# A chunked state-space scan: the next chunk's first segment sum and decay rows issued earlier, fp32r products regrouped

## The reference

```python
dAc = jnp.cumsum(dA, axis=-1)
seg = dAc[..., :, None] - dAc[..., None, :]
Lm = jnp.where(mask, jnp.exp(seg), 0.0)
Y_diag = jnp.einsum('bcqhn,bcshn,bhcqs,bcshp->bcqhp', Cm, Bm, Lm, xdt)
decay_states = jnp.exp(dAc[..., -1:] - dAc)
states = jnp.einsum('bcqhn,bhcq,bcqhp->bchpn', Bm, decay_states, xdt)
...
new = s + d[:, :, None, None] * carry
...
Y_off = jnp.einsum('bcqhn,cbhpn,bhcq->bcqhp', Cm, prevs, jnp.exp(dAc))
y = rmsnorm(y * jax.nn.silu(z), norm_w)
return y @ out_proj_w
```

## Time and profile before

| | us |
|---|---|
| runs: median of 3 (lowest to highest) | 1455.87 (1454.92 to 1456.91) |
| the profiled execution, its own time | 1456.05 |
| its span in the trace | 1453.9 |
| TensorE busy | 1385.4 (95%) |
| VectorE busy | 960.9 (66%) |
| ScalarE busy | 641.2 (44%) |
| GpSimd busy | 488.0 (34%) |

### The profile page before, as it was taken

The page is one execution under the profiler, slowest core; times in us unless marked ns, Lnnn a source line. Parts: engine busy times, 40 slices in busy tenths (PEclk is TensorE's granted clock), DMA queues, the critical chain, the costliest instruction groups (busy, mean ns, idle before and its releaser), DMA issues.

```text
span 1453.9 us, 20837 instructions
## 1 busy us (share of the span) xinstructions
PE 1385.4 (95%) x7268; PEld 1110.3 (76%) x7268; DVE 960.9 (66%) x1322; ACT 641.2 (44%) x1123; POOL 488.0 (34%) x479
## 2 busy tenths in 40 slices
PE   6899999989999997999999999999998789999997
PEld 4677777756666665888888888888886689999996
DVE  6879697789999996233333333233346879999996
ACT  4444454555555554221111121121212258888885
POOL 2612121247777675111010111010101336556652
PEclk9999999999999999999999999999999879999999
DMA  9133122833222222410000001020037724444433
GB/s 203 60 114 106 70 88 77 245 112 119 102 102 102 103 103 83 156 30 15 30 29 14 29 14 32 26 83 26 0 114 245 271 53 72 76 80 71 74 53 44
DMA packets 84360, 124.47 MB, mean 86 GB/s; under 512 B 27695, under 2 KB 44079, under 8 KB 84272
## 3 DMA queue, kind: packets, MB, share of 16 engines
q1 hardware_dynamic: 71488, 103.62, 21.8%
q0 software_dynamic: 8736, 18.62, 7.7%
q10 hardware_dynamic: 4048, 1.10, 0.3%
HBM read 81.37 MB, written 43.78 MB: 86 GB/s over the span
## 4 chain that ended last, share of the span: by engine, by line
PE 55%; DVE 2%; issue 1%; DMA 1%; ACT 1%; ACTq 0%; POOL 0%; DVEq 0%; POOLq 0%
PE fin_bank L1951 52%; PE fin_bank L2087 1%; DMA out_dram<-result_rows,put_idx 1%; PE fin_bank L2106 1%; PE fin_bank L2019 0%; PE fin_bank L2007 0%; PE fin_bank L2075 0%; DVE ff_w_lo L1736 0%; DVE onehot L1844 0%; ACT gu_hi L1632 0%; DVE fi_bn L1771 0%; DVE gu_lo L1863 0%; ACT ff_w_hi L1610 0%; ACTq L1337 0%; POOL out_dram L1564 0%
## 5 line engine op out<-in xcount | busy, mean ns | idle before, releaser
L1698 DVE TENSOR_TENSOR ff_prod<-ff_prod,fin_bank 128x512 f32<-128x512 f32 x64 | 44.0, 688 | 263.2 <-PE fin_bank L1951 263.2
L1951 PE MATMUL fin_bank<-ff_hT_hi,ff_w_hi 128*128 128x512 f32 x512 | 202.7, 396 | 3.2 <-DVE ff_w_lo L1706 3.2
L1951 PE MATMUL fin_bank<-ff_hT_lo,ff_w_hi 128*128 128x512 f32 x512 | 202.5, 395 | 0.0
L1951 PE MATMUL fin_bank<-ff_hT_hi,ff_w_lo 128*128 128x512 f32 x512 | 202.5, 395 | 0.0
L1450 POOL TENSOR_TENSOR ff_w_lo<-ff_stage,ff_w_hi 128x1024 fp32r<-128x1024 f32 (+1 forms) x24 | 56.5, 2356 | 410.6 <-ACT ff_w_hi L1600 406.2
L544 DVE SCALAR_TENSOR_TENSOR conv_acc<-raw,conv_w,conv_acc 128x512 f32<-128x512 f32 x144 | 115.7, 804 | 41.8 <-ACT raw L350 35.6
L649 PE MATMUL pj_bank<-hT_hi,w_in_hi 128*128 128x512 f32 x336 | 135.8, 404 | 6.9 <-POOL w_in_lo L297 4.2
L1585 ACT ACTIVATE ff_prod<-fin_bank 128x512 f32<-128x512 f32 x64 | 38.3, 598 | 231.2 <-PE fin_bank L1951 231.2
L649 PE MATMUL pj_bank<-hT_lo,w_in_hi 128*128 128x512 f32 x336 | 133.6, 398 | 0.0
L649 PE MATMUL pj_bank<-hT_hi,w_in_lo 128*128 128x512 f32 x336 | 132.7, 395 | 0.0
L1863 DVE TENSOR_TENSOR gu_lo<-wx,gu_hi 128x1408 fp32r<-128x1408 f32 (+1 forms) x79 | 124.9, 1620 | 1.6 <-ACT gu_hi L1632 1.6
(11 more groups left out here) (320 smaller groups left out, 3198.3 us busy)
## 6 DMA issues: line engine op xcount, KB each, us to landing
cv_rows<-cst SPq DMA_DIRECT2D x12, 1024.0 KB, 4.3
cv<-cv_rows SPq DMA_DIRECT2D x16, 768.0 KB, 4.2
zs_rows<-zst SPq DMA_DIRECT2D x8, 1024.0 KB, 6.5
zs<-zs_rows SPq DMA_DIRECT2D x16, 512.0 KB, 5.2
wx<-in_L_ffn_Wg_dram SPq DMA_DIRECT2D x8, 704.0 KB, 8.3
wx<-in_L_ffn_Wu_dram SPq DMA_DIRECT2D x8, 704.0 KB, 8.4
w_raw<-in_L_attn_in_proj_w_dram SPq DMA_DIRECT2D x32, 128.0 KB, 3.5
x<-_attn_hidden_states_dram SPq DMA_DIRECT2D x16, 256.0 KB, 5.4
```

What stands on the lines that cost most here:

```text
L1698: eng.tensor_tensor(prod[c][:, :], prod[c][:, :], up_ps[c][:, :], ALU.mult).then_inc(s["prod"], 1)
L1951: mm = eng.matmul(ps, w[a], x[b], start=first and i == 0, stop=last and i == 2)
```

## The change

In the lists of TensorE and ScalarE the first segment sum `seg(c + 1, 0)` with its exponentials and the first decay rows `cum_rows(c + 1, 0)` with theirs are issued at the end of pass c in place of the start of pass c + 1; on TensorE they stand right behind `out_proj(e, 1)` and ahead of the transposes `rows(c + 1)`. `seg(c, 2)` stands ahead of `diagonal(c, 0)` in place of behind it. On VectorE the two scores 0 and 1 follow each other, and `decayed_c(c, 0)` comes after both. No instruction is added or removed, and nothing changes on GpSimd and SyncE.

```diff
--- before.py
+++ after.py
@@ -938,12 +938,12 @@
                        .then_inc(s["wo_hi"], 1)
 
             rows(0)
+            exps(0, 0)
+            cum_exp(0, 0)
             for c in range(TILES + 2):
                 e, f = c - 1, c - 2
                 now, late, later = c < TILES, 0 <= e < TILES, 0 <= f
                 if now:
-                    exps(c, 0)
-                    cum_exp(c, 0)
                     exps(c, 1)
                 if c == 0:
                     out_high(0, HPG)
@@ -963,8 +963,11 @@
                     high(c, 0)
                     if c + 1 < TILES:
                         rows(c + 1)
+                        exps(c + 1, 0)
                 if late and now:
                     h_squares(e)
+                if c + 1 < TILES:
+                    cum_exp(c + 1, 0)
 
         @block.vector
         def _(eng):
@@ -1071,8 +1074,8 @@
                     gate(e, 1)
                 if now:
                     score(c, 0)
+                    score(c, 1)
                     decayed_c(c, 0)
-                    score(c, 1)
                 if c == 0:
                     out_low(0, HPG)
                 if late:
@@ -1217,19 +1220,19 @@
                 last.then_inc(s["h2T"], 1)
 
             rows(0)
+            seg(0, 0)
+            cum_rows(0, 0)
             for c in range(TILES + 2):
                 e, f = c - 1, c - 2
                 now, late, later = c < TILES, 0 <= e < TILES, 0 <= f
                 if now:
-                    seg(c, 0)
-                    cum_rows(c, 0)
                     b_dot_c(c, 0)
                     seg(c, 1)
                 if late:
                     out_proj(e, 0)
                 if now:
+                    seg(c, 2)
                     diagonal(c, 0)
-                    seg(c, 2)
                     carried(c, 0)
                 if late and now:
                     row_sums(e)
@@ -1241,6 +1244,9 @@
                     cum_rows(c, 1)
                 if late:
                     out_proj(e, 1, None if now else row_sums)
+                if c + 1 < TILES:
+                    seg(c + 1, 0)
+                    cum_rows(c + 1, 0)
                 if c == TILES:
                     turn_h2(f)
                 if now:
```

## The result

| | us |
|---|---|
| kernel before, 5 runs beside it: median (lowest to highest) | 1456.20 (1454.92 to 1457.49) |
| changed kernel, 5 runs: median (lowest to highest) | 1464.39 (1462.77 to 1464.83) |
| ratio, 95% interval | 1.0054, 1.0043 to 1.0065 |
| the profiled execution of the changed kernel, its span | 1464.39, 1462.3 |

A forecast was written before the change was run, and what follows sets the result against it. The prediction took a ring through TensorE, VectorE and GpSimd, ending with VectorE's squares, as the bound; 14 passes x 0.67 = 9.4 us on 1456.05 gave 1465.4, median 1465.2, own range 1462 to 1469, whole range 1454 to 1485.

The forecast's parts named there:

- The ring: One scan pass, from TensorE through VectorE's outcome, GpSimd and VectorE's squares back to TensorE's L1208; claimed to set its 17.32 us.
- The moved products: On TensorE, three fp32r products of 0.23 us ahead of the transposes; xdt starts later but ends as before, costing nothing.
- ScalarE's order: Moved exponentials ahead of h_squares on ScalarE make GpSimd's L861 wait, and the first L818 starts 0.67 us later.
- VectorE's order: Second score waits for its exponentials, decayed_c arrives 0.06 us ahead of the first L818, low is held; pass grows 0.67.
- the signs: Timeline marks of a right forecast, among them the second score waiting some 1.5 us and TensorE idle about 1.2 before L1208.
- The sum: Over the scan, 14 passes x 0.67 = 9.4 us slower, with nothing added for the opening.
- The opening: Chunks 0 and 1 of the scan, with waits of their own; given zero with 1 us to either side.
- The first rival: decayed_c comes after the first L818 starts, so both it and low are held; 1476 or 1485 us, chance 0.33.
- The fourth: Rival: the delays fit into the margins and the first L818 waits less than computed; 1456 us, chance 0.07.
- the second rival: low on VectorE isn't held and ends 0.16 us before its old time; -2.2 us, 1453.9, chance 0.09.
- the third rival: TensorE ends the pass; 0.33 us of wait and 0.22 of stretches go, 7.7 us faster, 1448, chance 0.06.

The follow-up runs named there:

- e5: The kernel before with only seg(c, 2) moved ahead of diagonal(c, 0) on TensorE, one fp32r stretch fewer; 1454.90 us, ratio 0.9987.
- e4: The changed kernel with h_squares back ahead of the exponentials and decayed_c back between the scores, products still moved; 1454.04 us, ratio 0.9982.
- e6: The changed kernel with GpSimd's two L818 products replaced by memsets that read nothing, leaving out the D x x term; 1451.45 us, ratio 0.9963.
- e1: The changed kernel with ScalarE's h_squares back ahead of the next chunk's exponentials; 1467.24 us, ratio 1.0074.
- e3: The changed kernel without VectorE's swap, decayed_c back between the two scores; 1445.99 us, ratio 0.9933.
- e2: The kernel before with VectorE's swap alone, the second score ahead of decayed_c; 1469.53 us, ratio 1.0091.
- e7: e3 with seg(c, 2) behind diagonal(c, 0) again, one fp32r stretch more; 1452.88 us, ratio 0.9969.

## Why the prediction was right, point by point

**The ring through GpSimd and VectorE's squares, not TensorE, ends the pass: right.** e5 and e4 shorten or move TensorE's work and leave the pass at 17.27; e6 touches only GpSimd and takes 0.83 off the changed kernel's.

**The moved products cost nothing: right.** Counted from the outcome, xdt began 0.69 later, as computed, and ended within 0.01 of its old place (3.18 against 3.19), and e4 has the old pass.

**ScalarE's order delays L818 by 0.67: right in size** (7.76 against 7.09 behind the outcome), and low ends as much later. Whether the kernel would be faster without the delay is another question, which the prediction ran together with the size. The gate's product stayed where it was (4.27 behind the outcome, before 4.28), as the step had it, and L863 ended 1.45 behind the end of that product, as read from the earlier trace rows. Against the real alternative, squares first, the late squares gain: 0.31 a pass with the swap (e1 to the changed kernel), 0.53 without it (e4 to e3), because GpSimd comes later and lets VectorE pass. So the 0.67 us are where the time stands in the trace, but taking them back makes the kernel slower.

**VectorE's order: right, and it is the cost.** L1013 arrived 0.07 ahead of L818 (0.06 computed), went first, and low was held to 1.53 us (1.5 computed). Two of the signs were mis-sized: the second score waited 1.09 us where "some 1.5" was written (the prediction's own chain gives 0.9), and the weight load of the row sums 0.99 where it was 1.2, as part of TensorE's waiting (0.33) came at `carried`. Without the swap the kernel is 18.4 us faster. The prediction never asked what this variant would do. With ScalarE's order as changed L863 ends later (on its own count 6.42 behind the outcome), and L1010, at its old place 6.12 behind it, starts ahead of L864 (6.51 on that count) and not in the middle of it.

**The sum: right, partly by chance.** 14 passes gave 9.3 us (9.4 computed). The opening was given zero with 1 us to either side and was worth -2.9, so this term failed. TensorE's timeline in the opening of the kernel before:

```profile
299.95 1.97 PE L1165 MATMUL ss_bank<-cexp,carry 64*64 64x128 f32 x16 [2.16 <-DVE cexp L1010]
301.86 1.97 PE L1176 MATMUL ss_bank<-xdd,xb_row 128*64 128x256 f32 x8
303.76 0.80 PE L1113 MATMUL ss_bank<-keep_mask_r,keep_ident_r 128*128 128x512 f32 x1
...
305.24 1.13 PE L1125 MATMUL ss_bank<-cv 64*128 64x512 f32 x4
```

Its clock there, with the columns of the earlier trace rows:

```profile
299.00:303.70 4.70, 3.75 (x24) 2.37 (x24) 4.35 (x7) 0.00 (x0) 0.97 (x1) 0.50 0.01 3
```

The granted clock is 0.50, the lower of the two levels (1.2 GHz), after TensorE had stood idle for 2.10 us ahead of `diagonal` and for 2.16 ahead of `carried`. TensorE's timeline of the changed kernel at the same place:

```profile
299.78 1.09 PE L1168 MATMUL ss_bank<-cexp,carry 64*64 64x128 f32 x16 [0.21 <-DVE cexp L1013]
300.80 1.08 PE L1179 MATMUL ss_bank<-xdd,xb_row 128*64 128x256 f32 x8
301.81 1.13 PE L1128 MATMUL ss_bank<-cv 64*128 64x512 f32 x4
```

`carried` and `states` come at a granted clock of 1.00 here and take 1.09 and 1.08 in place of 1.97 each; the next step starts 0.89 earlier behind either. The changed kernel has its low clock too, but earlier: its `diagonal` takes 1.97 us from 297.60, at a granted clock of 0.50 (1.09 from 296.70 before), after TensorE had stood idle for 2.02 us ahead of L1143. The three products had taken 1.48 us (303.76 to 305.24) and are gone from this place, and `carried` starts 0.17 earlier. Together the product of B and C starts 3.43 earlier (0.17 + 0.89 + 0.89 + 1.48); 2.9 of it are left at the row sums.

Against this the end of the scan and what follows took 2.0 us more. 0.5 of it lies ahead of the first feed-forward product (577.27 - 554.36 = 22.9 before, 584.14 - 560.75 = 23.4 after; L1219 at 579.80 lasted 1.11 there in place of 0.66, the granted clock being 0.62 in 579.00 to 581.00). 1.5 lies between that product and the end of the span (876.6 before, 878.2 after, and 878.0 in the changed kernel's second profile, 876.0 to 877.5 in the seven others). The first 13 feed-forward products took 5.64 us at a granted clock of 0.51, before 5.05 at 0.58, which is 0.6 of the 1.5. The other 0.9 stay open. So the 9.3 us of the passes were forecast for the right reason, but that the total came within about 1 us of it is luck: -2.9 and +2.0, neither in the sum, nearly cancel.

**The first rival: right in kind, mis-sized.** The double hold does happen in e1 and e2, at 0.97 a pass and not 1.45 above the kernel before, since an L818 that isn't itself kept waiting takes 1.04. With 1.04 in place of 1.48 for the first L818 its 1476 becomes 1470 (e2: 1469.5) and its 1485 about 1479, an estimate that no run tests. **The fourth** did not occur. **The second and third** needed low to be free. e6 frees it: a pass in the middle takes 17.15, 0.17 less than before, where the second rival had 0.16. e3 frees it and lets VectorE end earlier: 16.77, just the third rival's 17.32 - 0.55. But its two terms were both off: of the 0.33 us of wait only 0.16 went (the weight load still stands idle for 0.17 in e3, released by nobody), and the two stretches gave 0.39 (e4; 0.20 for one in e5) and not 0.22, since the end of a stretch costs about as much as its start. That the sum fits is luck.

What is shown and what isn't: that GpSimd's reading holds low is shown by e6. That the instruction that arrives first goes first fits every held pair shown here, and L985 and L835 were seen on both sides of it (0.16 ahead in e3, 0.05 behind in e7), though no run was made to test it. In the changed kernel L1013 goes first by 0.05 to 0.10 us in each of the 14 passes, in both of its profiles; what happens to L1013 on the other side was seen only with GpSimd's earlier times (e1, e2).

## What to carry to other kernels

Where GpSimd and VectorE both read two operands from SBUF, write their two lists side by side and look at who arrives first; an exchange of two VectorE instructions that changes no work moved this kernel by 13 us (e2) or 18 us (e3). Price a regrouping on TensorE only after showing that TensorE ends the pass: a stretch of fp32r products fewer was worth nothing in one order of VectorE's list (e5) and, with its knock-on, 0.36 us a pass in the other (e7). Try each part of a combined change by itself: the exchange of `decayed_c` and the second score, which adds no work, was the cost, and without it the rest is a gain (1446.0 against 1456.3).

## What the runs showed of the hardware that was not expected

- An SBUF to SBUF GpSimd product of 128 x 512 takes 1.04 us if it gets the ports at once and 1.49 if a VectorE product runs first: L818 with 1.04 and 1.49 in e1, and L835 with 1.04 (e7) and 1.49 (e3).
- A VectorE product that arrives 0.12 us before such a GpSimd instruction ends loses nothing: L1013 at 484.23 took 0.69 with L864 ending at 484.35.
- From a stretch of fp32r products to fp32 ones it is 0.33 us and not 0.23 (e7, L1119 to L1168), but to transposes 0.23 to 0.24 (L1143 at 476.79, L1189 at 477.03). A stretch that ends in fp32 products costs 0.20 us in all (the wait at the row sums grew from 0.32 to 0.52 in e5); one that ends in transposes would cost 0.1, an estimate from the two distances.
